# Expert projection with 118 stationary columns in place of 128 in a fused AdaLN and mixture-of-experts feed-forward kernel

## The reference

```python
# stage 1, per batch (16 batches of 512 tokens, 1024 features)
q_emb = relu(q @ W3 + b3)
x1 = (n * v + v_sum) * q_emb[:, None, :]
y = relu(x1 @ W2 + b2)
# stage 2, mixture of experts with E = 6 experts of rank R = 16, top 2
base_out = y @ W_base + b_base
shared_out = (y @ A_s) @ B_s
gates = softmax(y @ W_router + b_router)
w_per_e = top-2 gates, 0 for the other experts
h = einsum('bsd,edr->bser', y, A_r)
routed_out = einsum('bser,erf->bsf', h * w_per_e[..., None], B_r)
out = x + base_out + shared_out + routed_out
```

## Time and profile before

| | |
|---|---|
| time, median of 3 runs (lowest, highest) | 1448.36 us (1447.81, 1448.74) |
| the profiled execution: its time, its span in the trace | 1448.76 us, 1446.7 us |
| mean granted TensorE clock of the profiled execution | 0.996 |
| PE busy | 1429.2 us (99%), 6314 matmuls |
| PEld busy | 1168.9 us (81%), 6314 loads |
| DVE, ACT, POOL busy | 905.4, 677.9, 39.7 us |

### The profile page before, as it was taken

One profiled execution on the slowest core, in us unless ns is written; L12 is line 12 of the kernel. 1 busy time (PEld: TensorE's weight loads), 2 busy tenths in 40 slices (PEclk: granted clock), 3 DMA queues, 4 the chain that ended last, 5 costly groups with the idle time before them and its releaser, 6 DMA issues.

```text
span 1446.7 us, 18245 instructions
## 1 busy us (share of the span) xinstructions
PE 1429.2 (99%) x6314; PEld 1168.9 (81%) x6314; DVE 905.4 (63%) x1540; ACT 677.9 (47%) x1303; POOL 39.7 (3%) x71
## 2 busy tenths in 40 slices
PE   9889999999999999999999999999999999999999
PEld 5668888888888888888888888888888888888887
DVE  6966566564755647557788756565555646665564
ACT  6674674847658576585543232232322313132230
POOL 3130000000000000000000000000000000000000
PEclk9999999999999999999999999999999999999999
DMA  8231322413234232343653627246171542717242
GB/s 307 88 124 52 127 92 94 132 68 114 88 103 132 73 108 82 102 138 131 208 200 119 246 66 247 95 158 212 46 277 59 181 183 79 256 66 237 106 141 93
DMA packets 107229, 196.30 MB, mean 136 GB/s; under 512 B 12160, under 2 KB 12160, under 8 KB 107136
## 3 DMA queue, kind: packets, MB, share of 16 engines
q1 hardware_dynamic: 107136, 195.13, 39.8%
HBM read 123.78 MB, written 71.30 MB: 135 GB/s over the span
## 4 chain that ended last, share of the span: by engine, by line
PE 93%; DVE 3%; ACT 1%; issue 0%; POOL 0%; DVEq 0%; ACTq 0%
PE ps L1376 31%; PE ps L1378 31%; PE ps L1377 31%; DVE act_lo L930 1%; PE ps L1508 0%; DVE w_lo L916 0%; ACT src L575 0%; PE ps L1502 0%; DVE buf L975 0%; DVE src L962 0%; POOL w_hi L522 0%; DVE buf_lo L1010 0%; DVE wl_raw L1153 0%; DVE r L1135 0%; DVE src L968 0%
## 5 line engine op out<-in xcount | busy, mean ns | idle before, releaser
L1376 PE MATMUL ps<-act_hi,w_hi 128*128 128x512 f32 x1792 | 702.2, 392 | 4.2 <-issue 4.2
L1378 PE MATMUL ps<-act_hi,w_lo 128*128 128x512 f32 x1792 | 698.6, 390 | 0.0
L1377 PE MATMUL ps<-act_lo,w_hi 128*128 128x512 f32 x1792 | 698.4, 390 | 0.0
L1376 PEld LDWEIGHTS ps<-act_hi,w_hi 128*128 128x128 f32 x1792 | 337.1, 188 | 76.0 <-issue 5.0
L1378 PEld LDWEIGHTS ps<-act_hi,w_lo 128*128 128x128 f32 x1792 | 337.0, 188 | 70.7
L1377 PEld LDWEIGHTS ps<-act_lo,w_hi 128*128 128x128 f32 x1792 | 337.0, 188 | 69.0
L607 ACT ACTIVATE act_hi<-src 128x512 fp32r<-128x512 f32 x380 | 233.5, 623 | 258.5 <-PE ps L1378 256.8
L930 DVE TENSOR_TENSOR act_lo<-src,act_hi 128x512 fp32r<-128x512 f32 x320 | 220.3, 692 | 128.7 <-ACT act_hi L607 127.7
L975 DVE SCALAR_TENSOR_TENSOR buf<-ps,bb_sb,buf 128x512 f32<-128x512 f32 x128 | 95.7, 749 | 164.7 <-PE ps L1378 149.3
L975 DVE SCALAR_TENSOR_TENSOR buf<-ps,b_sb,buf 128x512 f32<-128x512 f32 x96 | 71.7, 749 | 66.2 <-PE ps L1378 65.8
L626 ACT ACTIVATE yhi<-buf 128x512 fp32r<-128x512 f32 x128 | 79.9, 625 | 39.1 <-PE ps L1378 38.9
(11 more groups left out here) (113 smaller groups left out, 997.1 us busy)
## 6 DMA issues: line engine op xcount, KB each, us to landing
src<-in_xT SPq DMA_DIRECT2D x224, 256.0 KB, 2.9
y_scratch<-buf SPq DMA_DIRECT2D x128, 256.0 KB, 2.1
src<-y_scratch SPq DMA_DIRECT2D x128, 256.0 KB, 5.1
outT<-buf SPq DMA_DIRECT2D x128, 256.0 KB, 4.3
buf<-in_xT SPq DMA_DIRECT2D x32, 256.0 KB, 4.5
wl_raw<-in_wbase SPq DMA_DIRECT2D x6, 1024.0 KB, 5.9
r<-in_w SPq DMA_DIRECT2D x16, 256.0 KB, 7.9
wh_raw<-in_wbase SPq DMA_DIRECT2D x3, 1024.0 KB, 8.1
```

The costliest lines, as they stand in the source:

```text
L1376: nc.tensor.matmul(out, wh, a_h, start=start, stop=False, skip_group_check=onto)
L1377: nc.tensor.matmul(out, wh, a_l, start=False, stop=False, skip_group_check=onto)
L1378: return nc.tensor.matmul(out, wl, a_h, start=False, stop=stop, skip_group_check=onto)
```

## The change

`AR` = 118 is new. In `project_y` and `turn_gates` the stationary operand has the first 118 columns of its block, and the output is 118 PSUM partitions. `copy_h` and `gate_apply` work on 118 partitions. Rows 118 to 127 of both `h_sb` tiles, which are still stored and later multiplied by zero rows, are set to zero once by two POOL memsets of the whole tiles; the first copy of each tile waits for both. The blocks in `a_hi`, `a_lo` and `wrow` keep their 128-column places.

```diff
+    AR = E + (E + 1) * R
     AC = P
...
+        h_set = sem("h_set")
...
                 nc.gpsimd.memset(earlier[:, e, 0:e], 1.0).then_inc(const_step, 1)
+            for w in (GB, GA):
+                nc.gpsimd.memset(h_sb[w][:], 0.0).then_inc(h_set, 1)
...
                 if i > 0:
                     act.wait_ge(hw_stored[w], 16 * i)
-                nc.scalar.activation(h_sb[w][:], ps[0:AC, H_BANK[w], :], ACT.Copy).then_inc(h_copied, 1)
+                else:
+                    act.wait_ge(h_set, 2)
+                nc.scalar.activation(h_sb[w][0:AR, :], ps[0:AR, H_BANK[w], :], ACT.Copy).then_inc(h_copied, 1)
...
-                nc.vector.tensor_tensor(h[:], h[:], ps[0:AC, H_BANK[w], :], ALU.mult).then_inc(hw_ready, 1)
+                nc.vector.tensor_tensor(h[0:AR, :], h[0:AR, :], ps[0:AR, H_BANK[w], :], ALU.mult).then_inc(hw_ready, 1)
...
-                cols = slice(f * AC, (f + 1) * AC)
-                three(ps[0:AC, H_BANK[w], :], a_hi[:, cols], a_lo[:, cols], yhi[:, s, :], buf[:, j, :],
+                cols = slice(f * AC, f * AC + AR)
+                three(ps[0:AR, H_BANK[w], :], a_hi[:, cols], a_lo[:, cols], yhi[:, s, :], buf[:, j, :],
...
-                    tr = nc.tensor.transpose(ps[0:AC, H_BANK[w], t * P:(t + 1) * P], wrow[:, t, :], ident[:])
+                    tr = nc.tensor.transpose(ps[0:AR, H_BANK[w], t * P:(t + 1) * P], wrow[:, t, 0:AR], ident[:])
```

More of the change, by code:

```diff
@@ L42, in adaln_ffn @@
     QK = condT.shape[1]
+    AR = E + (E + 1) * R
     AC = P
-    assert E + (E + 1) * R <= AC
+    assert AR <= AC
     TT = T // P
```

## The result

The changed kernel takes 1455.46 us (median of 6 runs, 1455.06 to 1456.28), the kernel before 1448.55 us beside it (6 runs, 1447.81 to 1449.6): a ratio of 1.0048, 95% interval 1.0035 to 1.0061. It is slower by 6.9 us; the span grew by 7.3 us, from 1446.7 to 1454.0. No change was forecast.

What follows compares the result with a forecast made beforehand. PE's matmul-to-matmul distance was taken to bound the kernel. The profiled 1448.76 us plus 0 for every term gave 1448.8, or 1448.4 us as a median, no change, with a range of 1445.2 to 1449.8 us.

Steps and rivals of the forecast that it cites:

- What bounds the kernel: Whole kernel: PE is busy 99% of the span, so only matmul-to-matmul distance or making PE wait can show.
- The 384 projection matmuls: Projection on PE: the load is hidden within the 227 ns pitch, so 0 us; bounds 4.2 us less to no change.
- Shared reads: Projection matmuls: moving and stationary reads share something, pitch 223.5 ns, 1.3 us less; kept in the likeliest case's range.
- the load sets the pitch: Projection matmuls: a just-late load makes the excess, up to 11 ns less each, 1443.7 us with transposes; chance 6 in 100.
- Another width is another shape: Projection: PE empties on entry and return, 410 ns per call, 52 us more, 1500.9 us; chance 5 in 100.
- A quick way of loading is lost: Projection loads: 118 columns lose a quicker load, 188 becomes 229 ns, 0.8 to 15.7 us more; chance 4 in 100.
- The gates' transposes: 64 transposes on PE: pitch stays 109 ns, 0 us; in proportion to columns at most 0.5 us less.
- ACT and DVE: Copies and products on 118 partitions: partitions cost nothing, 0 us; even 45 to 53 ns off would lie behind PE.
- the memsets: Two on POOL at the start: at most 1.07 us together, done by 3.1 us, hidden before POOL's work at 16.87.
- the wait: Ahead of the first copy of each h tile: first copy at 117.5 us, over 110 us after the memsets, costs 0.
- The range and the chances: Whole kernel: 1445.2 to 1449.8 us; no change 84 in 100, faster 7, slower 9.

Runs made afterwards that it cites:

- experiment 9: Kernel before, stationary operands at 128 columns, moving columns 512 down to 256 in pairs 8 to 15; pitch 173, 147, 120 ns at 384, 320, 256.

## Why the prediction was wrong

**What bounds the kernel** was right: PE's distance from start to start is what counts here, and the loss is in it.

**The 384 projection matmuls** is the step that failed. It set "no change: 0 us" as the upper bound and reasoned that a load which is hidden can't cost. The premises held (the loads start 2 to 4 ns after the matmul ahead and are done within the pitch, and they became 8 ns shorter), the conclusion didn't. The runs showed +60 ns per call (57 on the mean of all 128), +7.3 us in all, in place of 0 to -4.2. The bound had no row behind it on the side of a loss; the prediction said itself that no row had unequal widths in float32r, and it gave a loss 9 in 100, for two mechanisms that both did not happen.

The trace before did have a warning. Behind each group of transposes the matmuls of the same shape don't fall back to 227 ns at once. Three more rows of its timeline, right behind the earlier trace rows:

```profile
302.84 0.40 PE L1378 MATMUL ps<-act_hi,w_lo 128*128 128x512 f32 x1
303.07 0.40 PE L1376 MATMUL ps<-act_hi,w_hi 128*128 128x512 f32 x1
303.31 0.39 PE L1377 MATMUL ps<-act_lo,w_hi 128*128 128x512 f32 x1
```

By the stamps these starts and the one ahead of them are 229, 234 and 235 ns apart, then come 225, 230, 236, 229, 232 and 231, nine in all before 227 returns: within 1 ns the last seven are numbers seen behind a narrow projection. The prediction used the 340 ns of the first matmul and said nothing of the nine behind it. They suggest that 226.7 ns is a state that the engine keeps, and not a sum of costs, and so that what throws it out of step has a price behind it. The two states at 127 columns show that it is so there.

**Shared reads** (3.5 ns less per matmul), and **the load sets the pitch** (up to 11 ns less), the faster rival: neither. With 32 columns and a load 80 ns shorter the pitch is 231.7 ns, and with 256 moving columns the pitch is 120 ns under a load of 192.

**Another width is another shape**, the slower rival: right in sign, wrong in what happens and in size. There is no late load on entry or return (410 ns), but 60 ns in slower distances. Even 32 and 64 columns have no late load.

**A quick way of loading is lost**: no. The load of 118 columns took 180 ns against 188, and that of 127 took 187, so nothing was lost in it. Its price was unfounded as well: it began where the load outlasts the pitch of 227 ns, and a load that outlasts the pitch cost nothing in experiment 9. The rule of the Trainium skill, TensorE: Matmul & The Clock Gate, section on weight-path modes, would have had the narrower load come out longer if float32r counted as other than FP32; in this trace it came out shorter by the missing columns, so no sign of a quick load at 128 columns of float32r is seen here.

**The gates' transposes, ACT and DVE, the memsets, the wait**: right. The transposes keep 109 ns, the copy 577 ns, the memsets took 0.53 us each and ended at 2.9 us, and the kernel with all of these and a wide projection is at 0.9998. POOL's first rounding came at 17.59 us, not at 16.9, but it waited for the weights' transfer and not for the memsets, and the first projection started when it did before.

**The range and the chances**: 1445.2 to 1449.8 was built from the bound that failed, and 84 in 100 for no change was too sure for a step whose upper side had no row.

**What stays open.** That the loss comes from the projection's width alone, that it is paid in the pitch of matmuls which wait for nothing, and mostly behind the call, is shown. That one stream of equal matmuls can keep one pitch or another, by what went before, is shown at 127 columns. Why 128 settles at 13.3 ns over the stream, why 127 and 124 are free among wide neighbours and 126 is not, isn't: theory P, a point in time at which load and stream meet, missed at 126, at 127 and 124 everywhere, and in the size for one narrow load. Whether it is the narrower load or the narrower output couldn't be parted, since both come with one instruction here.

## What to carry to other kernels

In a stream of 512-column float32r matmuls at the upper clock, count the distance from start to start to the nanosecond, and keep the stationary operand at 128 columns: trimming it saved nothing at any width tried, though the load gets shorter. Used everywhere, narrower operands cost 1 to 7 ns per matmul here, and most widths cost 7 to 60 ns per interruption of three. If an operand must be narrower, try two or three widths near it; 124 was free where 118 cost 0.5%. For small transposes between large matmuls, try the full 128 rows, which was worth 0.09 us for each group of four here.

## What the runs showed that was not expected

- A disturbed stream of equal matmuls with 128 stationary columns recovers along one chain of distances (within 1 ns), 236, 224, 231, 236, 228, 233, 231, 226.7 ns, entered at different points after transposes, after narrow operands and at the start of the kernel.
- With 127 columns everywhere the stream keeps 233.3 ns for one stretch and 226.7 for another, some 10 us or longer each.
- At the lower clock there is no such chain and no excess: 512 columns take 427 ns with 128 stationary columns and with 118.
- 512 and 504 moving columns have the same pitch, 226.7 ns; 256, 320, 384 and 512 are 13.3 ns over the stream, 448 to 504 are 16.0 to 16.7.
- With 256 moving columns the loads last 192 ns, and the matmuls still start every 120 ns.
- The loads of 32 to 128 columns last 108 to 188 ns, 0.83 ns a column, and the pitch doesn't follow them.
